# First attention layer: in fourteen steps VectorE adds one head's mask, in place of a TensorE mask product

## The reference

```python
scores = jnp.einsum('bhqd,bhkd->bhqk', Q, K) / jnp.sqrt(jnp.float32(D_K))
scores = jnp.where(mask, -jnp.inf, scores)
attn_w = jax.nn.softmax(scores, axis=-1)
attn_w = jnp.where(jnp.isnan(attn_w), 0.0, attn_w)
out = jnp.einsum('bhqk,bhkd->bhqd', attn_w, V)
```

## Time and profile before

| | us |
|---|---|
| median of 3 runs | 1128.24 |
| lowest, highest | 1125.49, 1128.44 |
| profiled execution, its own time | 1122.69 |
| its span, first to last instruction | 1120.9 |

### The profile page before, as it was taken

One profiled execution on the slowest core, in us unless ns is written; L12 is line 12 of the kernel. 1 busy time (PEld: TensorE's weight loads), 2 busy tenths in 40 slices (PEclk: granted clock), 3 DMA queues, 4 the chain that ended last, 5 costly groups with the idle time before them and its releaser, 6 DMA issues. The chain is left out here.

```text
span 1120.9 us, 25280 instructions
## 1 busy us (share of the span) xinstructions
PE 1064.0 (95%) x10063; PEld 773.7 (69%) x10063; DVE 546.3 (49%) x1534; ACT 469.0 (42%) x738; POOL 486.6 (43%) x510
## 2 busy tenths in 40 slices
PE   7999999999899999999889999999985999999997
PEld 4555555544578788888765357555454999999997
DVE  4579888864831111111247887888454211112121
ACT  4467766766531111111052678888844111111110
POOL 4458888882066893000003444545503233333232
PEclk8999999999999999999989999999997999999999
DMA  8735222002547954435069522310007999999970
GB/s 215 176 99 96 45 45 45 3 3 86 203 151 196 338 199 171 149 141 138 3 214 244 92 46 45 61 29 3 2 30 218 380 376 347 316 322 313 303 248 2
DMA packets 90387, 170.68 MB, mean 152 GB/s; under 512 B 11814, under 2 KB 62200, under 8 KB 87848
## 3 DMA queue, kind: packets, MB, share of 16 engines
q1 hardware_dynamic: 81672, 157.50, 44.9%
q0 software_dynamic: 6048, 8.28, 3.1%
q10 hardware_dynamic: 2560, 3.41, 1.2%
HBM read 150.19 MB, written 19.54 MB: 151 GB/s over the span
## 5 line engine op out<-in xcount | busy, mean ns | idle before, releaser
L189 PE MATMUL s_ps<-k_stack,q_stack 97*32 97x512 bf16 x1904 | 210.7, 380 | 4.3 <-DMA q_stack<-q_scr 2.1
L1516 ACT ACTIVATE prob<-st_ps 128x1024 f32<-128x1024 f32 x186 | 189.6, 1022 | 58.9 <-PE st_ps L189 54.7
L189 PE MATMUL st_ps<-q_stack,k_stack 100*32 100x512 bf16 x2048 | 193.7, 379 | 2.2 <-ACTq L1486 0.9
L256 DVE CUSTOM_DVE_ANT_0 junk<-s_ps,bias_rows,mx 128x512 f32<-128x512 f32 x240 | 170.0, 748 | 27.4 <-PE s_ps L189 27.4
L256 DVE CUSTOM_DVE_ANT_0 junk<-s_ps,bias_rows 128x512 f32<-128x512 f32 x236 | 154.7, 688 | 39.0 <-PE s_ps L189 39.0
L1963 PE MATMUL h_ps<-expert_in,w 128*128 (+1 forms) x704 | 153.4, 379 | 2.7 <-DMA w<-in_w 2.0
L1403 PE MATMUL o_ps<-prob,v_unit 128*32 128x512 f32 x1024 | 143.9, 595 | 5.1 <-POOL prob L1315 3.4
L1963 PEld LDWEIGHTS h_ps<-expert_in,w 128*128 128x128 f32 (+1 forms) x704 | 131.4, 187 | 23.3 <-issue 3.3
L1315 POOL TENSOR_TENSOR prob<-prob,keep_cols 128x1024 int32<-128x1024 int32 x56 | 132.8, 2380 | 19.2 <-ACT prob L1516 18.9
L189 PEld LDWEIGHTS st_ps<-q_stack,k_stack 100*32 100x32 bf16 x2048 | 78.2, 97 | 71.9 <-issue 22.8
L189 PEld LDWEIGHTS s_ps<-k_stack,q_stack 97*32 97x32 bf16 x1904 | 73.2, 95 | 71.5 <-DVE mx L256 30.6
(11 more groups left out here) (363 smaller groups left out, 1453.4 us busy)
## 6 DMA issues: line engine op xcount, KB each, us to landing
wg<-in_gateT SPq DMA_DIRECT2D x23, 1024.0 KB, 6.3
wu<-in_upT SPq DMA_DIRECT2D x23, 1024.0 KB, 9.1
wd<-in_downT SPq DMA_DIRECT2D x23, 1024.0 KB, 12.5
w<-in_w SPq DMA_DIRECT2D x16, 1368.0 KB
w<-in_w SPq DMA_DIRECT2D x8, 1280.0 KB
k_stack<-k_scr SPq DMA_DIRECT2D x16, 384.0 KB, 5.2
k_stack<-k_scr SPq DMA_DIRECT2D x16, 256.0 KB, 5.6
k_scr<-k_parts SPq DMA_DIRECT2D x24, 128.0 KB, 2.8
```

The costliest lines, as they stand in the source:

```text
L189: mm = pe.matmul(out[cols], weights[:, cols], moving, start=start, stop=stop)
L256: self.pr.nc.vector.tensor_tensor_reduce(out=self.junk[:, self.bank("job", u, j)], in0=self.ps[:, self.bank("job", u, j)], in1=self.m.bias ...
L1516: nc.scalar.activation(prob[:, n % 2, 2 * hp:2 * hp + 2], st_ps[:, 2 * hp:2 * hp + 2], ACT.Exp).then_inc(exp_done, 1)
```

## The change

The constant `THIRD_AT = (2, 5)` names two steps of each unit. In layer 0, in the steps (u, 2) and (u, 5) of the units 0 to 6, head 2 becomes "unbiased": its mask product b2 is not issued, and its scores signal `third_ready`. VectorE does the first row job of the step (r0), then the new `third_mask`: it waits for `third_ready` and for the free half of `prob`, adds `bias_hi[:, kt]` to bank 2 of `st_ps` and writes the sum to `prob[..., 2]`; then come the other row jobs. ScalarE does the exponential of heads 0 and 1 as before, then that of head 3 alone from PSUM, then waits for `third_sum` and does that of head 2 in place in `prob`.

```diff
+THIRD_AT = (2, 5)
...
+            third_ready, third_sum = pr.sem("third_ready"), pr.sem("third_sum")
+
+        def third(u, kt):
+
+            return l == 0 and u < NU - 1 and kt in THIRD_AT
+
+        def thirds(u, kt):
+
+            return u * len(THIRD_AT) + THIRD_AT.index(kt) + 1
+
         def unbiased(u, kt, h):
 
             if u == NU - 1 and kt == KT - 1:
                 return False
+            if third(u, kt) and h == 2:
+                return True
             return h < (1 if l == 1 and u < NU - 1 else 2)
...
+                    elif alone and h == 2:
+                        mm.then_inc(third_ready, 1)
...
+                def third_and_fourth(u, kt):
+                    n = u * KT + kt
+                    act.wait_ge(st_ready, 2 * n + 2)
+                    nc.scalar.activation(prob[:, n % 2, 3], st_ps[:, 3], ACT.Exp)
+                    act.wait_ge(third_sum, thirds(u, kt))
+                    nc.scalar.activation(prob[:, n % 2, 2], prob[:, n % 2, 2], ACT.Exp).then_inc(exp_done, 1)
...
+                        elif third(u, kt):
+                            exps(n, 0)
+                            third_and_fourth(u, kt)
...
+                def third_mask(u, kt):
+                    n = u * KT + kt
+                    dve.wait_ge(third_ready, thirds(u, kt))
+                    dve.wait_ge(pv_done, n + 1)
+                    nc.vector.tensor_tensor(prob[:, n % 2, 2], st_ps[:, 2], m.bias_hi[:, kt],
+                                            ALU.add).then_inc(third_sum, 1)
+
                 for u in range(NU):
                     for kt in range(KT):
-                        row.maxima(dve, plan[u, kt])
+                        row.maxima(dve, plan[u, kt][:1])
+                        if third(u, kt):
+                            third_mask(u, kt)
+                        row.maxima(dve, plan[u, kt][1:])
```

## The result

| | before | after |
|---|---|---|
| median, us (20 runs each, in one comparison) | 1125.55 | 1128.12 |
| lowest, highest | 1122.67, 1131.72 | 1124.76, 1133.14 |
| profiled execution's own time | 1122.69 | 1125.74 |
| its span | 1120.9 | 1124.0 |

The ratio after to before is 1.0026, interval 1.0013 to 1.0038. The forecast was 0.5 us less. The time is in the forecast range and within 0.3%, yet it moved the other way: with 20 runs a side, 0.26% can be told from nothing.

The account below looks back on a forecast made before the run. TensorE's gapless stream was taken as the bound. Odd units -0.1, steps 5 and 6 -0.75 and unit 0 +0.37 summed to -0.5 us, giving a median of 1127.7 us, range 1124.6 to 1131.0.

Parts of the forecast that it names:

- TensorE's stream is the bound of unit 1: Unit 1: PE busy 24.40 of 24.40 us without a gap, so TensorE's stream sets the time.
- The odd units give 0.1: Units 1, 3, 5, steps 2 and 3: T waits for VectorE, 0.04 of 0.217 us is left; three times, -0.1.
- steps 5 and 6 give 0.75: Units 1 to 5, steps 5 and 6: weigh at 124.91 in place of 125.06, -0.15 us; five times, -0.75.
- Even units 0: Units 2, 4, 6, step 3: weigh waits for POOL anyway, saving and T's delay both vanish; zero, three times.
- unit 6 0: Unit 6, step 5: POOL paces, so zero.
- Unit 0 loses 0.37: Unit 0: VectorE has no pause, the add delays T and weigh; +0.2 us from step 2, +0.17 from step 5.
- The add takes 0.69: VectorE's added 128 x 512 operation in the fourteen steps: 0.69 us, no overlap into the next; bounds 0.61 and 1.22.
- the exponentials 0.598 and 0.62: ScalarE's split pair: 0.598 us from PSUM, 0.62 in place; about 0.2 us more per step, room 0.25, no cost.
- The bank wait does not bind: Rival, chance 0.18: VectorE makes up its lateness, nine places keep the whole product, 1.95 us saved, median 1126.3.
- The add costs more than the product saves: Rival, chance 0.15: VectorE's lateness delays T at ten places; add of 1.0 us gives +2.6, 1.22 gives +4.8.
- shifts elsewhere: Outside the changed steps: stretches where PE's stops are put down to nothing the profile shows; chance 0.05.

Follow-up runs that it names:

- the removal alone: Changed kernel without VectorE's add and ScalarE's split, b2 and head 2's mask left out in the fourteen steps: 1127.11 us, ratio 1.0011.
- the add alone: Kernel before plus VectorE's add into a spare tile, b2 kept, ScalarE waiting for the add: 1127.78 us, ratio 1.0008.
- refilled profiles: Changed kernel with four 16-column matmuls in place of each b2: ratios 0.9999, 0.9991, 0.9990; same in steps 3 and 7, units 1 to 6: 0.9994.
- the lengthened kernel before: Kernel before with the same 14 x 4 tiny matmuls added in front of head 2's scores, b2 kept: 1125.29 us, ratio 0.9986.

## Why the prediction was right or wrong

*TensorE's stream is the bound of unit 1.* Half right. Beside it ran a GpSimd chain of the same length over each pair of a changed step and its turn (`keep`, `cut`, `keep`, weigh: 6.24 us from weigh to weigh, in either kernel). I saw POOL's 21.34 of 24.40 busy and its hold of the weigh in even units, and did not follow its chain in the odd ones.

*The odd units give 0.1, steps 5 and 6 give 0.75.* Wrong, both are 0; this is the step of the sum that failed. Its DVE part was good: T of (1,3) came at 115.54 where I had 115.64. What it left out is GpSimd: the weigh waits for `keep` as well, and I let T alone set it. T of (1,6) came 0.23 earlier than before, its weigh 0.10, and 0.10 is what the whole unit stood earlier (the weigh of (1,1) at 109.44 and 109.54). That GpSimd is enough to hold it is shown by the removal alone: no add on VectorE, 163.33.

*Even units 0, unit 6 0.* Right. The weigh of (2,3) idles 0.45 us for POOL after, 0.48 before:

```profile
140.86 1.06 PE L1418 MATMUL o_ps<-prob,v_unit 128*32 128x512 f32 x8 [0.45 <-POOL prob L1328]
```

*Unit 0 loses 0.37.* Right in mechanism and in the releaser of T in (0,3), a little small: the weigh of (0,3) is 0.23 later than before (0.2 forecast), that of (0,6) another 0.25 (0.17 forecast), 0.48 in all; shown by the add alone.

*The add takes 0.69, the exponentials 0.598 and 0.62.* Right as lengths; the lines of the changed kernel:

```profile
L1598 DVE TENSOR_TENSOR prob<-st_ps,bias_hi x14: 681/686/687, 85.1 to 245.7; 128x512 f32<-128x512 f32 x14
L1537 ACT ACTIVATE prob<-st_ps x14: 593/597/601, 84.8 to 246.4; 128x512 f32<-128x512 f32 x14
L1539 ACT ACTIVATE prob<-prob x14: 622/630/637, 85.8 to 246.9; 128x512 f32<-128x512 f32 x14
```

The next maximum starts 0.60 us behind the add (112.09, 112.69), below its own 0.69. I took 0.69 with no overlap; 0.60 was outside my lower bound of 0.61 by a hair. The Trainium skill, VectorE: DVE Perf Modes, "The DRAIN you can't avoid", says that the next operation waits for the pipeline to empty, and adds that one which is not held starts earlier. The prediction gave only the first half; the 0.60 beside 0.69 agrees with the addition.

*The rivals.* "The bank wait does not bind" had its premise come nearly true in step 6 (T at 124.67, 0.09 behind its place in the stream) and not its 1.95 us, since POOL binds. "The add costs more than the product saves" fell: no more than 0.69. The sum of the attention is then +0.5 where I had -0.5, from these terms alone.

*What was no term.* The prediction put everything outside the changed steps at nothing, with a chance of 0.05 for "shifts elsewhere", and that is the second step that failed. Of the 1.9 us at equal clock (the first comparison's 2.6 us and the 2.1 of all five ratios are not distinguishable from it) 0.5 is the attention's own and 1.4 is such a shift. Shown in the whole time: programs with the shorter TensorE stream lose 1.3 us at equal clock whatever their attention does, and with the number of instructions put back, the changed steps as they are, the loss is not there. Shown in place: the stop in unit 0, which ends 1.50 to 1.65 us behind the end of a packet of code, in seven of ten shorter programs and in none of the four refilled profiles; and a packet of code in the last stage, behind which weights land 1.3 us later, at a cost of 0.5 to 0.9 us where no fall of the clock covers it. Open: what moves the packets, so that the lengthened kernel before, with a packet in the last stage and no stop in unit 0, loses nothing; and how much of the 1.3 us lies in the last stage, since three of four refilled profiles are as long there as the changed kernel's. So which places a shift of the code hits is not a rule that these runs give.

## What to carry to other kernels

Before a product is taken off a full TensorE, follow each other engine's chain over the same two or three steps. An engine that is only 87% busy can have a chain just as long as the stream there, and then the product saved brings nothing: the pair of steps with the turn was such a place, the step without one (step 7) was not. A trade is tested first by its removal alone: where that gains nothing, no cheaper replacement will. An effect of 0.1 to 0.2% is no larger than what a changed program length shifted elsewhere here: to read it, put the length back with tiny instructions, take many runs, and compare at equal mean clock. And read a place in all profiles of a kernel: the first of the refilled kernel alone would have said that its last stage is as short as before's.

## What the runs showed of the hardware

The transfer queue for instructions carried 74 packets (1.21 MB) before and 73 (1.20 MB) after:

```profile
q8 instruction: 73, 1.20, 0.5%
```

That is some 270 matmuls and weight loads to a packet, an estimate from 20,126 of them and 74 packets, if all packets are TensorE's; the change takes away 112. At 0.5% of the transfer engines' time the queue looks like nothing, yet behind one packet in a stretch where weights take 85% of them a tile's weights landed about 1.3 us later, and TensorE stopped in the middle of a product until 1.50 to 1.65 us behind the end of another. Executions of the kernel before in the five rounds lay up to 13 us apart (1119.29 to 1132.38), most of it the clock.
